# Attention with rope: from the third batch on, the exchanged halves come from DMA copies of the projection instead of a second product with turned weights

## What is computed

```python
qkv = x @ w_qkv
q, k, v = jnp.split(qkv, 3, axis=-1)
...
def _apply_rope(x, cos, sin):
    half = x.shape[-1] // 2
    x1, x2 = (x[..., :half], x[..., half:])
    return jnp.concatenate([x1 * cos - x2 * sin, x2 * cos + x1 * sin], axis=-1)
q = _apply_rope(q, cos, sin)
k = _apply_rope(k, cos, sin)
scores = jnp.einsum('bhqd,bhkd->bhqk', q, k) * scale
...
attn = jax.nn.softmax(scores, axis=-1)
out = jnp.einsum('bhqk,bhkd->bhqd', attn, v)
...
return out @ w_out
```

## Time and profile before

| | us |
|---|---|
| median of 3 runs (lowest, highest) | 1030.18 (1030.01, 1031.18) |
| the profiled execution's own time | 1031.45 |
| its span in the trace | 1029.7 |
| busy PE, PEld, DVE, ACT, POOL | 790.1, 519.1, 680.8, 511.1, 430.4 |
| attention, first to last product of its maxima (L1420) | 544.0 to 866.0 |

### The profile page before, as it was taken

One profiled execution on the slowest core, in us unless ns is written; L12 is line 12 of the kernel. 1 busy time (PEld: TensorE's weight loads), 2 busy tenths in 40 slices (PEclk: granted clock), 3 DMA queues, 4 the chain that ended last, 5 costly groups with the idle time before them and its releaser, 6 DMA issues.

```text
span 1029.7 us, 18855 instructions
## 1 busy us (share of the span) xinstructions
PE 790.1 (77%) x5628; PEld 519.1 (50%) x5628; DVE 680.8 (66%) x2458; ACT 511.1 (50%) x1374; POOL 430.4 (42%) x497
## 2 busy tenths in 40 slices
PE   4689883988499950599748888988988998728977
PEld 3578872647398750377632233333433333316757
DVE  4555555775855539555497677888888887565634
ACT  5323331605043313766311466767767678676660
POOL 1047772400277753311176457566475533261100
PEclk9999997895599985699985588988989899969998
DMA  5831113002011131000032332141232200000002
GB/s 150 238 72 49 49 48 94 1 1 82 15 47 50 49 72 37 0 1 1 1 62 30 52 44 44 29 59 33 34 56 30 44 2 4 2 0 0 2 1 83
DMA packets 53427, 42.97 MB, mean 42 GB/s; under 512 B 9861, under 2 KB 48722, under 8 KB 53328
## 3 DMA queue, kind: packets, MB, share of 16 engines
q1 hardware_dynamic: 46784, 31.74, 15.0%
q0 software_dynamic: 4992, 9.32, 3.3%
q10 hardware_dynamic: 1552, 0.70, 0.3%
HBM read 18.27 MB, written 11.40 MB: 29 GB/s over the span
## 4 chain that ended last, share of the span: by engine, by line
PE 44%; DVE 18%; issue 13%; ACT 10%; POOL 9%; DMA 4%; ACTq 1%; DVEq 0%; SPq 0%; POOLq 0%
PE psum L1448 6%; POOL arena L823 5%; PE psum L1433 4%; PE psum L1388 3%; ACT arena L1606 3%; PE psum L1219 3%; PE psum L740 3%; PE psum L1182 3%; PE psum L1191 2%; DVE cst L1513 2%; PE psum L1420 2%; DMA result_rows<-arena,scatter_row 2%; PE psum L1282 2%; DVE half_stats L441 2%; POOL arena L1064 2%
## 5 line engine op out<-in xcount | busy, mean ns | idle before, releaser
L1513 DVE CUSTOM_DVE_ANT_0 cst<-psum,rot 128x512 bf16<-128x512 f32 (+3 forms) x512 | 222.7, 486 | 54.1 <-PE psum L1420 48.8
L1606 ACT ACTIVATE arena<-psum 128x512 f32<-128x512 f32 (+1 forms) x384 | 177.9, 533 | 61.3 <-PE psum L1433 54.5
L823 POOL DMA_INDIRECT arena<-xhat_rows,gather_row x78 | 77.1, 989 | 154.3 <-DVE scatter_row L640 131.1
L1420 PE MATMUL psum<-arena 48*128 48x512 bf16 (+3 forms) x512 | 123.2, 334 | 17.1 <-DVE row_max L1513 15.9
L1433 PE MATMUL psum<-arena 51*128 51x512 bf16 (+3 forms) x512 | 113.7, 318 | 12.0 <-ACT arena L1606 7.9
L1697 POOL TENSOR_SCALAR_AFFINE_SELECT arena<-arena 128x384 f32<-128x384 f32 x128 | 63.6, 521 | 129.5 <-ACT arena L1606 129.5
L1448 PE MATMUL psum<-arena 128*32 128x512 f32 (+3 forms) x1024 | 100.4, 492 | 1.9 <-POOL arena L1700 1.9
L831 POOL DMA_INDIRECT result_rows<-arena,scatter_row x78 | 78.2, 1002 | 31.6 <-issue 22.0
L790 PE MATMUL psum<-arena 128*128 x624 | 90.8, 289 | 0.1
L778 PE MATMUL psum<-arena 128*128 128x128 f32 x624 | 87.3, 285 | 1.7 <-DVE arena L652 1.6
L711 ACT ACTIVATE arena<-psum,gate_b1T 128x128 f32<-128x128 f32 x156 | 48.9, 364 | 65.3 <-PE psum L778 65.3
(11 more groups left out here) (249 smaller groups left out, 1688.9 us busy)
## 6 DMA issues: line engine op xcount, KB each, us to landing
arena<-cut SPq DMA_DIRECT2D x192, 64.0 KB
xhat_rows<-xh SPq DMA_DIRECT2D x16, 256.0 KB, 2.3
arena<-result_rows SPq DMA_DIRECT2D x8, 512.0 KB, 6.1
x<-in_L_attn_x SPq DMA_DIRECT2D x4, 512.0 KB, 7.4
arena<-in_L_ffn_w SPq DMA_DIRECT2D x1, 2048.0 KB, 9.9
out<-x SPq DMA_DIRECT2D x4, 512.0 KB, 3.2
arena<-xhat_rows,gather_row POOLq DMA_INDIRECT x78, 2.5
result_rows<-arena,scatter_row POOLq DMA_INDIRECT x78, 2.3
```

The lines of the kernel that those rows point to most:

```text
L823: pool.indirect_dma_start(xg[:, j % AHEAD, :], None, xhat_dram, bass.IndirectOffsetOnAxis(gather_row[:, j:j + 1], 0)).then_inc(gathered[j ...
L1420: mm = pe.matmul(to[:, col:col + (k + 1) * P], q_stack[b % STACKS][rows, h, k * P:k * P + P], k_stack[b % STACKS][rows, h, 0:(k + 1) * P], ...
L1513: last = nc.vector.tensor_tensor_reduce(masked_scores[:, number % 2, col:col + n_keys], frm[:, col:col + n_keys], mask[:, S - n_keys:], 1. ...
L1606: nc.scalar.activation(prob_e[g % 2][:, j, first:last], bank[MAX_BANKS + number % EXP_BANKS][:, 0:last - first], ACT.Exp, scale=DH ** -0.5 ...
```

## The change

For batches 0 and 1 nothing changes. For batches 2 to 7 the jobs s0 and s1 are gone and p1 moves from slot 13 to slot 12. After the copy of a projection to `raw`, ScalarE issues four DMAs; each copies 32 partitions of `raw` (64 KB) to the 32 partitions of `swapped` where their exchanged half belongs. VectorE multiplies `swapped` by `sin` in place, in SBUF, behind the maxima of slot 14 (queries) and of slot 15 (keys). GpSimd's op 0, which overwrites `raw`, waits for the copies as well (`halves_in`). The lines of the changed kernel are numbered 2 to 14 higher.

```diff
@@ the list of jobs
                 else:
-                    at_body, at_slot = (b - 2,) * 5, (10, 11, 12, 13, 14)
+                    at_body, at_slot = (b - 2,) * 5, (10, 11, 12, 12, 13)
                 for step, i, slot in zip(steps_in, at_body, at_slot):
-                    JOBS[i].append((slot, step, b))
+                    if b < 2 or step[0] != "s":
+                        JOBS[i].append((slot, step, b))
@@ VectorE
+                def sines_of_halves(b, r):
+
+                    dve.wait_ge(halves_in[r], 64 * (b - 1))
+                    nc.vector.tensor_tensor(swapped[:, r, :], swapped[:, r, :], sin, ALU.mult).then_inc(sines[r], 1)
+
...
                         for step, b, m in jobs_at(i, hh):
                             job(step, b, m)
+                        if 0 <= i and i + 2 < B and hh in (14, 15):
+                            sines_of_halves(i + 2, hh - 14)
@@ ScalarE, job p
                         nc.scalar.copy(raw[:, r, :], bank[misc_bank(m)][:]).then_inc(raw_in[r], 1)
                         act.wait_ge(raw_in[r], b + 1)
                         act.sem_inc(s["misc_read"], 1)
+                        if b >= 2:
+                            for q in range(4):
+                                act.dma_start(swapped[32 * (q ^ 1):32 * (q ^ 1) + 32, r, :], raw[32 * q:32 * q + 32, r, :]).then_inc(halves_in[r], 16)
@@ GpSimd, rotate
                     if op == 0:
                         engine.wait_ge(raw_in[m], b + 1)
+                        if b >= 2:
+                            engine.wait_ge(halves_in[m], 64 * (b - 1))
                         issue.tensor_tensor(v, v, cos, ALU.mult).then_inc(turned_in[m], 1)
```

More of the change, by code:

```diff
@@ L1299, in attention @@
             raw_in = [sem(f"a{n}_raw_in{i}") for i in range(2)]
+            halves_in = [sem(f"a{n}_halves_in{i}") for i in range(2)]
             stack_in = [sem(f"a{n}_stack_in{i}") for i in range(2)]
```

## The result

| | before | after |
|---|---|---|
| median, us (lowest, highest) | 1030.10 (1025.51, 1031.18), 4 runs | 1078.44 (1077.35, 1079.27), 4 runs |
| profiled execution, own time | 1031.45 | 1078.49 |
| span | 1029.7 | 1076.8 |

The ratio is 1.0469, with a 95% interval of 1.0453 to 1.0485: 48 us more, where 39 were forecast. The span grew by 47.1 us. Between the first and the last start of a maxima slot of attention lie 362.8 us instead of 317.9, so 44.9 of the 47.1 are there. By bodies, from slot 0 to slot 0: body 0 takes 44.6 us (44.9 before), bodies 1 to 4 take 49.5 to 50.2 (39.3 to 41.4 before), body 5 takes 48.7 (40.9) and body 6 takes 38.8 (36.3). The prediction had looked for 44 to 48 in bodies 0 to 5 and for no change in body 6; the wait for the mask of batch 5 falls into body 6.

What follows compares the result with a forecast made beforehand. No engine was full; a ring of TensorE, ScalarE and VectorE, with GpSimd's mask 2.0 us ahead, bounded the kernel. 5 x 6.5 + 3.0 + 3.0 = 38.5 us on 1031.45, less 1.3, gave 1069 us, range 1050 to 1084.

Steps and rivals of the forecast that it cites:

- Both mechanisms: ScalarE's issues delay exponentials, and GpSimd's masks wait behind the late queries' multiplication: together 6.5 us late a body.
- ScalarE alone: Issues ahead of the exponentials in slots 12 and 13 make the next body start 3.4 us late.
- GpSimd's chain: GpSimd's queue from op 1 to `causal(3, 1)`, 8.84 us, waits for slot 14's multiplication; slot 1's sums wait for its end.
- the prediction's sum: Whole kernel: five bodies at 6.5, body 0 at 3.0, plus 3.0 for clock and contention: 38.5 us.
- ScalarE's term: ScalarE's queue, slots 12 and 13: four issues take 2.64 us ahead of the exponentials; next body 3.4 late.
- the two prices: Cost of one DMA issue on ScalarE: 0.45 us from its loads, or 0.66 from SP's SBUF copies, the one taken.
- GpSimd's term: Slot 1's sums wait for the mask, 6.5 us late a body, 3.2 later than ScalarE's issues would make it.
- 0.5 a body: Addition for TensorE's lower clock in slots 12 to 15 and SBUF contention: 3.0 us in all, bounds 0 to 2.5.
- the first rival: Issues on ScalarE cost little, only GpSimd's queue counts: about 1040 us, or 1059 at 0.45 an issue; chance 0.08.
- 1.5 us a body: Slots 12 to 15: most that removing two products and the waits behind the multiplications could gain, if nothing hindered.
- Costed at nothing: Landing of the SBUF copies, with 4 us of cover, and SP's query-part copies, a body ahead of use: no cost.
- the ring: TensorE, ScalarE and VectorE share three banks each way; a delay of any longer than a slot's slack delays all.

Runs made afterwards that it cites:

- run 1: Changed kernel with SP issuing all eight copies of a batch and ScalarE none: 1045.93 us, ratio 1.0165.
- run 2: Changed kernel with the queries' multiplication behind slot 13 instead of slot 14, issues still on ScalarE: 1054.34 us, ratio 1.0241.
- run 4: Kernel before plus eight DMA issues a batch on ScalarE, small copies that nobody reads: 1046.38 us, ratio 1.0176.
- run 3: Kernel before, turned products kept, with VectorE's multiplications moved to slots 14 and 15, no added copies: 1050.01 us, ratio 1.0196.
- run 11: Changed kernel with the keys' multiplication moved from slot 15 into slot 1 of the next body: 1077.42 us, ratio 1.0463.
- run 8: Kernel before, products kept, with GpSimd's masks ahead of the queries' rotation and SP's part copies later to match: 1043.21 us, ratio 1.0110.
- run 9: Changed kernel with SP issuing the copies and only GpSimd's ops 3 to 5 of the queries behind `causal(i, 1)`: 1048.85 us, ratio 1.0180.
- run 6: Changed kernel with GpSimd's masks ahead of the queries' rotation, issues still on ScalarE: 1063.39 us, ratio 1.0320.

## Why the prediction was right, and where it was short

**Both mechanisms, each by itself and both ways.** "ScalarE alone" and "GpSimd's chain": taking away the one gives 32.5 us back (run 1), the other 24.1 (run 2); adding the one to the kernel before costs 17.3 (run 4), the other 20.9 (run 3). The two additions make 38.2 us, almost the 38.5 of the prediction's sum, and the change costs 48.3.

The 10 us between them don't come from the two losses meeting. Run 2 has the issues without the late multiplication, and costs 25.3 us, already 8.0 more than run 4, where the same issues stand in the kernel before. The rows of body 4 say what differs: in run 4 TensorE makes p1 in slot 13 and s1 in slot 14 (1.12 and 1.13 us, s1 while ScalarE issues), waits 1.87, 1.35 and 0.46 us for exponentials from slot 12 on, and its sums of slot 14 take 0.85; in run 2 neither product stands in those slots, it waits 1.85, 2.07 and 0.61 us, and the same sums take 1.51 at the lower clock. That fits products that covered a part of the issues' time while they were there. The place of the second group of issues, a slot earlier in run 2, the missing products and the clock were not told apart by a run.

**ScalarE's term.** Forecast: 2.64 us for four issues, slot 14 3.7 us late. The median issue of 612 ns with its gap makes 2.45 for four, and with the wait 2.66 up to the exponentials. For slot 14, body 4 is the clean one to read:

```profile
777.18 0.69 DVE L1515 CUSTOM_DVE_ANT_0 cst<-psum,rot 128x512 bf16<-128x512 f32 x1 [0.74 <-PE psum L1422]
781.18 0.69 DVE L1515 CUSTOM_DVE_ANT_0 cst<-psum,rot 128x512 bf16<-128x512 f32 x1 [1.81 <-PE psum L1422]
785.83 0.69 DVE L1515 CUSTOM_DVE_ANT_0 cst<-psum,rot 128x512 bf16<-128x512 f32 x1 [2.92 <-PE psum L1422]
```

Slots 12 and 13 take 8.65 there and 708.55 - 703.59 = 4.96 in the kernel before: 3.7 late, as forecast. In body 3 it is 4.7, since one of the eight issues took 1.62 us. The choice between the two prices, SP's 0.66 and the 0.45 of ScalarE's loads, was right; the lower one is refuted by 48 issues with none under 514 ns. The Trainium skill's 50 ns of dispatch (DMA: Bandwidth & Descriptors, "Anatomy of one DMA") stands in a section on DMAs that GpSimd issues, which the prediction didn't say; for ScalarE these 48 issues decide.

**GpSimd's term.** Forecast 3.2 us of waiting a body over what ScalarE alone would do, measured 3.01 in body 3. The chain was put at 8.84 and takes 749.14 - 739.76 = 9.38, the 0.54 more being the two mask operations of 1.53 instead of 0.99. They start with the keys' multiplication (742.35 both). So the Trainium skill's rule (SBUF - State Buffer, "Who interferes with whom") holds here, but the prediction drew the wrong consequence from it: it let the multiplication wait for GpSimd, off the path, and GpSimd waited for the multiplication, on the path. Run 11 shows the 0.5 us following the multiplication. VectorE lost as well, off the path: the cast of slot 15 (L1527, one SBUF input, 128x32), 0.20 us in the kernel before, starts at 741.68 beside GpSimd's op 2 of 741.12, takes 0.75 and ends 0.04 behind it; that is 0.55 of the 1.5 us by which slot 15 grew. The prediction's "while one with a single SBUF input doesn't" leaves out that the page excepts casts in some modes.

**The term that was mis-sized** is the last of the sum, "0.5 a body" for clock and contention, inside its own bounds of 0 and 2.5. From the start of slot 12 to the sums of slot 1 the kernel before takes 13.75 us and the changed one 21.50 in bodies 2, 4 and 5: 7.75 more, where the forecast was 6.5 + 0.5. Up to slot 14 nothing is off. Slot 14, up to the end of its multiplication, took 0.64 longer than forecast, since its sums, put at 0.85, take 1.51 at 1.2 GHz; the chain took 0.54 longer by contention. Together 1.2 a body instead of 0.5. The prediction expected the clock to fall for lack of work in slots 12 to 15, gave the price of these sums as up to 0.9, and weighted it too low.

Two smaller misses make up the rest. The long issues in bodies 1 and 3 add 1.3 and 1.0 us, which no term had, and body 0 was put at 3.0 late and is 4.1. So 5 x 1.2 + 2.3 + 1.1 = 9.4 stand where the sum had 3.0: 38.5 becomes 44.9, which is what attention grew by from its first to its last maxima slot. The other 2.2 us of the span's 47.1 lie outside these slots, where the change does nothing; the runs differ there by as much (attention starts between 545.8 and 550.1 us).

**Slips in the working.** L1738 is not the one row of before in which VectorE multiplies or adds two SBUF tiles: at 522.94 to 527.74 four more stand beside GpSimd's ops (L1743, L1745, L1747 and L1749, VectorE's share of a rotation) and take 1.52 to 1.64 us, GpSimd's 1.48 to 1.78. They were a warning that 0.69 might not hold; it did hold, at 677 to 690 ns in the changed kernel. In the first rival, at 0.45 an issue, 24 + 3.0 leaves body 0 at its full lateness, and 1031.45 + 27 + 3 - 1.3 is 1060 and not 1059. Neither changes the forecast.

**What was granted to the change.** The "1.5 us a body" of the removal: in run 1 slots 12 to 14 take 2.3 to 2.4 us less than before (2.0 forecast), but slot 15 gives back 1.2 to 1.5 instead of 0.69, so slots 12 to 15 take 9.4 to 9.6 us instead of 10.4. In body 0 they take 9.5 instead of 12.7, a gain of 3.1 us that the prediction had not seen; with ScalarE issuing it is eaten up. No kernel that was run turned this into a time below that of the kernel before.

**Costed at nothing:** the landing of the copies, rightly so with ScalarE issuing (2.0 us, well ahead of the multiplication), not with SP issuing, where op 0 ran into the multiplication; and SP's copies, rightly so in the changed kernel (weight loads wait 3.6 us for the maxima's rows, once, against 4.2 before), but runs 8 and 9 show how near they are to the path, by the bytes in flight in the one and by the order of the queue in the other.

## What to carry to other kernels

A DMA issue is an instruction of the engine that issues it: count it at 0.6 us of that engine's queue and ask what stands behind it, however small the copy. An operation that is moved takes with it everything that is queued behind its consumer, here 8.8 us of GpSimd work behind a multiplication of 0.69. And in a pipeline with a few hundred nanoseconds to two microseconds of margin at several places, curing one late wait by reordering shows the next (the mask, then the row copies): read every queue that is shared by what you move, and what the DMA engines are still carrying when a small copy is issued.

## What the runs showed of the hardware that was not expected

- The issue of a copy within SBUF takes 612 ns by the median on ScalarE and 614 (stack parts) or 590 (run 1's copies of `raw`) on SP, with 256 bytes a partition as with 2048. The loads on ScalarE's queue in this kernel took 0.41 to 0.60.
- Single issues took 1.1 to 1.9 us. In ScalarE's queue they are not random: of the 48 copies of `raw` the 14th and the 30th are the longest in the changed kernel (1.90 and 1.62), in run 2 (1.45 and 1.24), run 6 (1.82 and 1.35) and run 11 (1.56 and 1.37), while run 4's 48 small copies have none above 0.92. On ScalarE the ring is held up by the excess: slots 12 and 13 take 9.93 and 9.67 us in bodies 1 and 3 of the changed kernel and 8.66 in the others behind body 0. SP has such issues too (1.53 in the kernel before). The cause is open.
- In the VectorE and GpSimd contention the one that starts later loses, in the cases read here whose order can be told: masks of 0.99 us took 1.49 and 1.53 beside a multiplication of two SBUF tiles, ops of 1.27 took 1.68 and 1.80, while the multiplication kept to 676 to 689 ns in all twelve cases of run 1; and VectorE's cast of 0.20 us took 0.75 beside a GpSimd op that had started before it.
- In run 8 two copies of 12 KB that SP issued at once, up to 616.18, reached TensorE at 623.22, 7.0 us later, behind 24 copies of 64 KB.
